# Scores of four heads formed in two pairs, and evictions moved behind the scores

## The reference

```
h = layernorm(x) * (1 + ca) + sa                 # x: 8 x 512 x 128
k, v, q = split(h @ w_in.T)                      # 16 heads of width 8
logits = q @ k.T / sqrt(8) + bias[head]          # 512 x 512 for each head and batch
out = softmax(logits) @ v
x = x + ga * out
```

## Time and profile before

| | us |
|---|---|
| median of 3 runs | 2723.67 (2720.2 to 2725.59) |
| profiled execution | 2719.2 |
| its span in the trace | 2717.5 |
| first to last score of the attention stage | 114.2 to 925.1 |

### The profile page before, as it was taken

How to read it: one execution, slowest core, us unless ns; L and a number is a source line. 1 busy time by engine, 2 the same in 40 slices (tenths; PEclk the granted TensorE clock), 3 DMA queues, 4 the chain that set the end, 5 groups by cost and what they waited for, 6 DMA issues and landing times. The chain is left out here.

```text
span 2717.5 us, 63728 instructions
## 1 busy us (share of the span) xinstructions
PE 2174.8 (80%) x25656; PEld 1389.3 (51%) x25656; DVE 1854.9 (68%) x4420; ACT 1443.6 (53%) x2943; POOL 793.0 (29%) x851
## 2 busy tenths in 40 slices
PE   2698888888888757468898998888989875687984
PEld 1244444444444436246666666666666654455652
DVE  2477767776675523678989988889998882682333
ACT  0377666666665512746666666666666644232221
POOL 1000001001000125124444444344444442103884
PEclk9599899998897869669888888888998897698997
DMA  5000000000000043100000000000000001333334
GB/s 185 33 1 5 5 5 8 5 5 9 5 5 5 9 124 91 47 9 10 12 12 12 12 12 12 12 12 12 12 12 13 4 4 51 111 110 93 44 43 87
DMA packets 109526, 85.53 MB, mean 31 GB/s; under 512 B 22366, under 2 KB 97282, under 8 KB 108976
## 3 DMA queue, kind: packets, MB, share of 16 engines
q1 hardware_dynamic: 95664, 68.31, 8.6%
q0 software_dynamic: 13568, 13.14, 2.9%
HBM read 59.22 MB, written 22.71 MB: 30 GB/s over the span
## 5 line engine op out<-in xcount | busy, mean ns | idle before, releaser
L617 ACT ACTIVATE Pr<-Pr,nmax 128x512 f32<-128x512 f32 x512 | 341.2, 714 | 179.0 <-DVE nmax L552 176.8
L722 PEld LDWEIGHTS bank<-ident,Pr 128*128 128x128 f32 x2048 | 247.9, 154 | 259.8 <-DVE PT L561 153.1
L722 PE MATMUL bank<-ident,Pr 128*128 128x128 f32 x2048 | 321.5, 302 | 71.8 <-DVE PT L561 58.9
L552 DVE CUSTOM_DVE_ANT_0 Pr<-bank,Tb 128x512 f32<-128x512 f32 x512 | 331.1, 685 | 45.1 <-PE bank L708 45.0
L561 DVE COPY PT<-bank 128x512 f32<-128x512 f32 x256 | 176.5, 689 | 192.4 <-PE bank L736 188.2
L2454 PE MATMUL bank<-Wcv,hw 128*128 128x512 f32 x512 | 264.1, 663 | 13.0 <-ACT bank L2261 7.4
L624 ACT ACTIVATE PT<-bank 128x512 f32<-128x512 f32 x256 | 150.9, 589 | 120.0 <-PE bank L736 85.1
L2084 DVE TENSOR_TENSOR Tc<-Tc,pr 128x30 f32<-128x30 f32 (+14 forms) x480 | 200.8, 418 | 16.5
L2083 DVE TENSOR_TENSOR pr<-AC,Tc 128x30 f32<-128x30 f32 (+14 forms) x480 | 183.2, 382 | 17.4 <-POOL Tc L1954 3.6
L708 PE MATMUL bank<-kp,qp 8*128 8x512 f32 x1024 | 179.8, 701 | 1.1 <-DVE nmax L552 1.1
L2454 PEld LDWEIGHTS bank<-Wcv,hw 128*128 128x128 f32 x512 | 103.5, 214 | 129.2 <-issue 117.6
(11 more groups left out here) (404 smaller groups left out, 4495.1 us busy)
## 6 DMA issues: line engine op xcount, KB each, us to landing
aB<-alpha SPq DMA_DIRECT2D x64, 128.0 KB, 2.9
Tb<-scores SPq DMA_DIRECT2D x1, 7168.0 KB
w<-in_L_ffn_W SPq DMA_DIRECT2D x16, 256.0 KB, 5.8
rawW<-in_L_ffn_up_w SPq DMA_DIRECT2D x16, 256.0 KB, 2.9
rawW<-in_L_ffn_gw SPq DMA_DIRECT2D x16, 256.0 KB, 3.3
rawW<-in_L_ffn_down_w SPq DMA_DIRECT2D x16, 256.0 KB, 4.0
disp<-zero SPq DMA_DIRECT2D x1, 2580.0 KB, 16.3
xin<-disp SPq DMA_DIRECT2D x8, 322.5 KB, 6.3
```

The costliest lines, as they stand in the source:

```text
L552: V.tensor_tensor_reduce(out=Pr[:, s, i, :], in0=pS[hh][:, :], in1=Tb[:, h, at:at + L], scale=-1.0, scalar=3.0e38, op0=ALU.add, op1=ALU.mi ...
L617: A_(Pr[:, s, i, :], Pr[:, s, i, :], ACT.Exp, scale=-1.0, bias=nmax[:, s, i:i + 1])\
L722: last = TR(pT[m % 2][:, t * P:(t + 1) * P], Pr[:, (G % 2) * HG + hh, t, j * P:(j + 1) * P], ident[:, :])
```

## The change

TensorE does the scores of heads 0 and 1 first, then transposes m and m+1, then the scores of heads 2 and 3, then transposes m+2 and m+3, values and misc. VectorE does score 0, 1, evac m, score 2, 3, evac m+2. ScalarE does expo 0, evac m+1, expo 1, 2, evac m+3, expo 3. The number of instructions, their shapes, the buffers and the waits stay as they were.

```
--- before.py
+++ after.py
@@ -565,16 +565,16 @@
                     for R in range(END):
                         b, p = R // 16, R % 16
                         m = (R - LT) * HG
-                        if 0 <= m < NR * HG:
-                            evac(m)
                         if R < NR:
                             score(R * HG)
                             score(R * HG + 1)
                         if 0 <= m < NR * HG:
-                            evac(m + 2)
+                            evac(m)
                         if R < NR:
                             score(R * HG + 2)
                             score(R * HG + 3)
+                        if 0 <= m < NR * HG:
+                            evac(m + 2)
                         if p == 0 and b + 1 < B:
                             normed(b + 1)
                         for kind, x in at_round(R):
@@ -635,15 +635,16 @@
                         m = (R - LT) * HG
                         if R >= 9 and (R - 9) % 4 == 0 and (R - 9) // 4 < B * NG:
                             take((R - 9) // 4)
+                        if R < NR:
+                            expo(R * HG)
                         if 0 <= m < NR * HG:
                             evac(m + 1)
                         if R < NR:
-                            expo(R * HG)
                             expo(R * HG + 1)
+                            expo(R * HG + 2)
                         if 0 <= m < NR * HG:
                             evac(m + 3)
                         if R < NR:
-                            expo(R * HG + 2)
                             expo(R * HG + 3)
                         for kind, x in at_round(R):
                             misc(kind, x)
@@ -696,12 +697,12 @@
                                 last = TR(pM[:, t * P:(t + 1) * P], oT[:, x % 2, t * P:(t + 1) * P], ident[:, :])
                         last.then_inc(r["b_mm"], 1)
 
-                    def scores(R):
+                    def scores(R, heads):
                         G, i = R // LT, R % LT
-                        if i == 0:
+                        if i == 0 and heads[0] == 0:
                             pe.wait_ge(r["b_pm"], USE[("q", G)] + 1)
                             pe.wait_ge(r["b_pm"], USE[("k", G)] + 1)
-                        for hh in range(HG):
+                        for hh in heads:
                             if R:
                                 pe.wait_ge(r["b_s"], (R - 1) * HG + hh + 1)
                             rows = slice(32 * hh, 32 * hh + HD0)
@@ -739,11 +740,13 @@
                         misc(kind, x)
                     for R in range(END):
                         m = (R - LT) * HG
+                        if R < NR:
+                            scores(R, (0, 1))
                         if 0 <= m < NR * HG:
                             transposes(m)
                             transposes(m + 1)
                         if R < NR:
-                            scores(R)
+                            scores(R, (2, 3))
                         if 0 <= m < NR * HG:
                             transposes(m + 2)
                             transposes(m + 3)
```

## The result

The changed kernel is slower: 2762.76 us median (2761.22 to 2764.25, 4 runs) against 2721.93 (2717.91 to 2725.59, 4 runs), a ratio of 1.0158 with a 95% interval of 1.0123 to 1.0194. Forecast were 2798 us in a range of 2745 to 2850, and slower. The sign and the mechanism held; of the +75 us that the sum gave, the medians show +41.

The account below looks back on a forecast made before the run. TensorE was taken to lead, with no engine full. Batches 2 to 6 +54 us, batch 1 +7, batch 0 +10 and batch 7 +4 made +75: span 2793, median 2798 us, range 2745 to 2850.

Parts of the forecast that it names:

- A pair costs as much as four heads: TensorE's scores: each pair takes 1.07 us, adding that to each of 128 rounds, 137 us at full clock.
- The rival in which a pair costs half: A pair of score heads takes 0.54 us, so nothing is added; total 2716 us, faster; chance 4%.
- The waits that come back: TensorE's waits for evictions get covered: 9.6 us a batch returns against 17.1 added, 7.5 slower at full clock.
- The list's other entries: Full-clock rounds p of a batch: o (p = 6, 10, 14), spread (7), T and r (0), c (2), deviation (9).
- p = 1: The batch's round with the t job: 5.64 us at full clock.
- p = 8 (v): The batch's round with the v job, estimated as a job like k: 6.15 us at full clock.
- The list as a whole: All rounds of one of batches 2 to 6 summed at full clock: 102.3 us, against 94.8 before.
- The clock of batches 2 to 6: 22% of the time at half clock, mean 0.89: 115 us a batch, +10.8 each, +54 for five.
- The 0.87 to 0.91: Sign to look for afterwards: the mean granted clock of batches 2 to 6 lies in this range.
- my rival with the clock as before: Only the waits matter, clock stays 0.91: 112.4 us a batch, +8.2, total 2785 us; chance 33%.
- The last batch: Batch 7, without q, k, t, v: 93 us at full clock, some 118 at an unchanged clock of 0.78, +4.
- Batches 0 and 1: Batch 0, first four rounds scores alone in two blocks: +10 us; batch 1, without T, r, c: 101 us, +7.

Follow-up runs that it names:

- values_pairs: values_between with its scores cut into the two pairs of the change, the second behind the values: 2731.36 us, ratio 1.0067.
- values_between: Changed kernel with all four heads' scores first, values between the two halves of the transposes, and VectorE reordered to match: 2570.55 us, ratio 0.9469.
- before_early: Kernel before, with ScalarE copying the transposed rows (T) ahead of expo 2 and 3 instead of behind them: 2687.47 us, ratio 0.9912.
- pairs_only: TensorE as in the changed kernel, VectorE and ScalarE in the order of the kernel before: 2809.38 us, ratio 1.0346.
- after_filled: Changed kernel with one matmul whose result nobody reads in TensorE's wait between T and r: 2770.78 us, ratio 1.0218.

## Why the prediction was right, and where its size was off

- **A pair costs as much as four heads.** Right: 1.05 to 1.06 us from start to start, forecast 1.07. values_pairs against values_between shows it in the whole time. The rival in which a pair costs half is out.
- **The waits that come back.** Right: the evictions start where the sum had them, 2.38 after the first pair and 1.13 after the values; rounds are 5.18 and 6.20 us. The list's other entries, read from VectorE's first scores of successive rounds: o 6.00 (5.97), p = 7 7.16 in the one batch of the five where the clock stays up there (7.2), p = 0 8.85 (8.9), p = 2 7.22 (7.2). p = 9 was 6.45 to 7.9, forecast 7.5. p = 1 had a mean clock of 0.63 and took 8.15 where the list at full clock has 5.64, and p = 8 (v) had 0.78 in every batch and took 7.85, forecast 6.15. The list as a whole held: 109.3 us less half of the 17 us at half clock is 100.8 (an estimate), forecast 102.3.
- **The clock of batches 2 to 6.** This is the first term that was mis-sized. I took 22% of the time at half clock, since "scores, 8 rows deep, stand around it twice, and the stops at p = 2, 7 and 9 stay". The mean clock was 0.92, 16%. The sum with that share, 102.3 / 0.92 = 111, is near the 109.3 measured; the forecast 115 made 54 us of what was 25. The 0.87 to 0.91 that I had named as a sign was missed too, and my rival with the clock as before (2785) was the nearer one. No run separates what the depth of the scores does to the clock. With a second block of them it was 0.93 in values_pairs instead of 0.98, but 0.92 in the changed kernel, where waits went as well, instead of 0.91.
- **The last batch.** The second: I kept its 0.78 "at the same 0.78 divided by 0.78" and had +4. It had 0.89 and -16 us. Nothing in the list tells it; the experiment does. In before_early, too, T to r is short and this batch takes 99.2 us; in pairs_only T to r is long and it takes 120.6. The shorter wait, which I had worked out to 0.1 us, goes with a second yield in the clock, and I had counted only the waiting. By how much is less sure: with the order of before this batch took 107.1 to 114.0 us in three executions.
- **Batches 0 and 1** were +12.0 and +11.8, forecast +10 and +7.
- **Outside the stage** I kept the time. The profiled executions differ by 11.5 us there, and after_filled, with the changed attention, has a recurrent attention 16.1 us shorter than the changed kernel's, so this is not put down to the change. It brought the total nearer to the forecast by luck: the stage was to take 75 us more and took 33.

Of the profiled executions' 44.4 us, then, 33 are the stage's: 12.0 + 11.8 + 25.1 - 16.0. What in each batch still brings the clock down in the changed kernel I have not settled. The longest stretch at half clock stands behind T and r, but filling most of the idle time there left it as it was.

## What to carry to other kernels

Matmuls that run side by side on row tiles are one block: count blocks, not heads, before cutting such a group to fill a wait, and look first for work that is whole already (here the values) to put in its place. When an order on one engine and one on another are tied by a wait, price both together: the evictions' order alone cost 13%, and one block of scores less gave nothing as long as evac m stood behind two scores. A wait on TensorE can have two prices, the waiting and the clock behind it. In the kernel before, a cheap edit that shortened the longest one was worth two to three times its microseconds; in the changed kernel and in values_between, filling the same wait gave nothing.

## What was not expected of the hardware

Two matmuls per batch whose result is thrown away made the kernel faster by 1.0% (0.9898, 0.9866 to 0.9929), with a mean clock of 0.94 instead of 0.91. With a wait of 2 us in each round of 7 us, half of the time ran at 1.2 GHz (mean 0.75). And a stage of 1.2 ms with the same instructions took between 1203.6 and 1221.0 us in executions whose earlier work differed little.
